# Attention with three DMA-joined pairs of blocks, values in half-blocks, and TensorE's program written out

## The reference

```python
dots = jnp.einsum('bhnd,bhmd->bhnm', q, k) * SCALE          # 2 x 16 heads, 2048 x 2048, head width 32
attn = jax.nn.softmax(dots, axis=-1)
out  = jnp.einsum('bhnm,bhmd->bhnd', attn, v)
```

## Time and profile before

| | us |
|---|---|
| median of three executions | 1948.23 |
| the profiled execution: its time | 1950.18 |
| the profiled execution: its span | 1948.4 |
| attention in it | about 318 to 1422 |
| TensorE busy | 1814.7 (93%) |
| VectorE busy | 1456.9 (75%) |
| ScalarE busy | 1448.6 (74%) |
| GpSimd busy | 161.3 (8%) |

### The profile page before, as it was taken

The page is one execution under the profiler, slowest core; times in us unless marked ns, Lnnn a source line. Parts: engine busy times, 40 slices in busy tenths (PEclk is TensorE's granted clock), DMA queues, the critical chain, the costliest instruction groups (busy, mean ns, idle before and its releaser), DMA issues. The chain is left out here.

```text
span 1948.4 us, 38894 instructions
## 1 busy us (share of the span) xinstructions
PE 1814.7 (93%) x14516; PEld 845.0 (43%) x14516; DVE 1456.9 (75%) x1579; ACT 1448.6 (74%) x1572; POOL 161.3 (8%) x131
## 2 busy tenths in 40 slices
PE   8999996999999999999999999999939996899786
PEld 6777772333333333333333333333327774444332
DVE  5443435888888888888888888888826776688687
ACT  5343445999999999999999999999905654555475
POOL 0000000000000000000000000000011220000164
PEclk9999998999999999999999999999969996899898
DMA  8655654536446364463555354463653520133274
GB/s 293 224 202 199 221 194 166 109 91 151 92 113 145 75 145 113 89 159 80 114 140 108 88 151 94 110 148 75 143 184 135 182 93 1 60 141 156 80 281 167
DMA packets 111553, 268.57 MB, mean 138 GB/s; under 512 B 7956, under 2 KB 26516, under 8 KB 101780
## 3 DMA queue, kind: packets, MB, share of 16 engines
q1 hardware_dynamic: 98324, 193.05, 27.4%
q0 software_dynamic: 9216, 67.11, 18.6%
q10 hardware_dynamic: 3968, 7.86, 1.1%
HBM read 115.95 MB, written 84.93 MB: 103 GB/s over the span
## 5 line engine op out<-in xcount | busy, mean ns | idle before, releaser
L783 DVE TENSOR_TENSOR dve_sum<-dve_sum,probs 128x2048 f32<-128x2048 f32 x320 | 732.8, 2290 | 80.7 <-ACT probs L699 73.1
L699 ACT ACTIVATE probs<-score_others,shift_now 128x1536 f32<-128x1536 f32 x384 | 622.0, 1620 | 0.0
L840 PE MATMUL score_first<-q_parts,k_parts 32*128 32x512 f32 x1542 | 494.1, 425 | 24.2 <-DMA v_group<-v_scratch 11.6
L840 PE MATMUL score_others<-q_parts,k_parts 32*128 32x512 f32 x4626 | 499.0, 426 | 0.0
L840 PEld LDWEIGHTS score_first<-q_parts,k_parts 32*128 32x128 f32 x1542 | 245.0, 183 | 492.2 <-ACT probs L698 288.0
L868 PE MATMUL mixed_ps<-probs,v_group 128*32 128x512 f32 x3072 | 395.9, 603 | 2.9
L698 ACT ACTIVATE probs<-score_first,shift_now 128x512 f32<-128x512 f32 x384 | 291.1, 758 | 43.0 <-PE score_others L840 43.0
L840 PEld LDWEIGHTS score_others<-q_parts,k_parts 32*128 32x128 f32 x4626 | 252.6, 183 | 2.2
L699 ACT ACTIVATE probs_joined<-score_others,shift_now 128x1536 f32<-128x1536 f32 x128 | 199.9, 1562 | 0.0
L812 POOL DMA_DIRECT2D probs_joined<-probs_joined x64 | 55.2, 863 | 1040.7 <-PE mixed_ps L868 1010.7
L868 PEld LDWEIGHTS mixed_ps<-probs,v_group 128*32 128x32 f32 x3072 | 67.1, 108 | 160.2 <-issue 110.0
(11 more groups left out here) (206 smaller groups left out, 2181.9 us busy)
## 6 DMA issues: line engine op xcount, KB each, us to landing
probs_joined<-probs_joined POOLq DMA_DIRECT2D x64, 1024.0 KB, 8.6
k_parts<-k_scratch SPq DMA_DIRECT2D x36, 512.0 KB, 4.8
q_parts<-q_scratch SPq DMA_DIRECT2D x33, 512.0 KB, 7.8
o_scratch<-out_parts SPq DMA_DIRECT2D x33, 512.0 KB, 2.8
h_scratch<-h SPq DMA_DIRECT2D x6, 2816.0 KB, 8.1
h<-h_scratch SPq DMA_DIRECT2D x6, 2816.0 KB, 10.5
k_scratch<-parts SPq DMA_DIRECT2D x32, 512.0 KB, 3.6
q_scratch<-parts SPq DMA_DIRECT2D x32, 512.0 KB, 2.7
```

Source lines behind the costliest of these rows:

```text
L699: nc.scalar.activation(block_probs(k)[:, CH:HPG * CH], score_others[n % 2][:], ACT.Exp, bias=shift[:, c:c + 1], scale=SCALE).then_inc(prob ...
L783: nc.vector.tensor_tensor(total[:], first[:], block_probs(k)[:], ALU.add).then_inc(dve_added, 1)
L840: last = nc.tensor.matmul(out, k_parts[rows, a, k * P:(k + 1) * P], q_parts[c][rows, b, :], start=t == 0, stop=t == len(TERMS) - 1)
```

## The change

Three pairs of blocks are now joined by DMAs: (0, 1), (4, 5) and (10, 11). Only the sum of the last goes to a ones-group of its own (`TO_SUMS`). The sums of the other two are read by VectorE as two of its twelve operands (`ADD_ORDER`), so that it still makes eleven additions. There are two ones-groups for each chunk instead of three: the joined pair in step 0, `dve_sum` in step 1 (`SUMS_AT`). VectorE reads the sums (`finish`) before its first addition of a chunk, no longer after it. The values are issued in halves of 256 columns: `VALUE_HALVES` says how many halves a step takes. Steps 2 and 3 take blocks 0 and 1. Steps 4, 7, 10 and 13 take three halves. Blocks 3, 4, 5, 10, 11 and 12 are split over two steps, the others are issued whole. The ring for single blocks has five tiles instead of six. `normal` is gone (the product is written into `mixed`), and `out_parts` is single instead of double, with one `stored` semaphore. TensorE's program has no loop: all 32 chunks are written out, and the two scores past the end are left out.

```diff
-    JOINED = (8, 9, 10, 11)
-    ADDED = [k for k in range(KB) if k not in JOINED]
-    ADDS = len(ADDED) - 1
-    P_RING = len(ADDED) // 2
+    PAIRS = ((0, 1), (4, 5), (10, 11))
+    TO_SUMS = (2,)
+    ADD_ORDER = (2, 3, 6, 7, 0, 8, 9, 4, 12, 13, 14, 15)
+    SUMS_AT = ((0,), (1,))
     W_SLOT = 4
+    SINGLE = [k for k in range(KB) if not any(k in pair for pair in PAIRS)]
+    ADDS = len(ADD_ORDER) - 1
+    P_RING = len(SINGLE) // 2
     AHEAD = 2
-    VALUES_AT = [[], [], [0], [1, 2], [3], [4, 5]] + [[k] for k in range(6, KB)]
+    VALUE_HALVES = (0, 0, 2, 2, 3, 2, 2, 3, 2, 2, 3, 2, 2, 3, 2, 2)
+    HALF = CH // 2
...
-            return probs_joined[JOINED.index(k)] if k in JOINED else probs[ADDED.index(k) % P_RING]
+            i = pair_of(k)
+            return probs[SINGLE.index(k) % P_RING] if i is None else probs_paired[i][PAIRS[i].index(k)]
+        def pair_of(k):
+            return next((i for i, pair in enumerate(PAIRS) if k in pair), None)
+        def added_at(k):
+            return max(ADD_ORDER.index(k), 1)
...
-                            if k in JOINED:
+                            i = pair_of(k)
+                            if i in TO_SUMS:
                                 act.wait_ge(sums_done, it * CPB + c + 2)
-                            elif ADDED.index(k) >= P_RING:
-                                act.wait_ge(dve_added, (it * CPB + c + 1) * ADDS + max(ADDED.index(k) - P_RING, 1))
+                            elif i is not None:
+                                act.wait_ge(dve_added, (it * CPB + c) * ADDS + added_at(PAIRS[i][0]))
+                            elif SINGLE.index(k) >= P_RING:
+                                act.wait_ge(dve_added, (it * CPB + c + 1) * ADDS + added_at(SINGLE[SINGLE.index(k) - P_RING]))
                             else:
-                                act.wait_ge(dve_added, (it * CPB + c) * ADDS + ADDED.index(k) + P_RING)
+                                act.wait_ge(dve_added, (it * CPB + c) * ADDS + added_at(SINGLE[SINGLE.index(k) + P_RING]))
...
+                        take_shift(it if c == 0 else it + 1, (c + CPB - 1) % CPB)
+                        finish(it, c)
                         for a in range(ADDS):
-                            k = ADDED[a + 1]
-                            n = c * KB + k
-                            if a == 1:
-                                take_shift(it if c == 0 else it + 1, (c + CPB - 1) % CPB)
-                                finish(it, c)
                             if a == ADDS - 1:
                                 gather(it, c + 1)
-                            v.wait_ge(probs_done, (it + 1) * EXPS + (n + 1) * 2)
+                            k = ADD_ORDER[a + 1]
+                            if pair_of(k) is None:
+                                v.wait_ge(probs_done, (it + 1) * EXPS + (c * KB + k + 1) * 2)
+                            else:
+                                v.wait_ge(joined[pair_of(k)], 16 * (it * CPB + c + 1))
                             if a == 0:
                                 v.wait_ge(sums_done, 1 + it * CPB + c)
-                                first = block_probs(ADDED[0])
+                                first = block_probs(ADD_ORDER[0])
...
-                for i in range(2):
-                    nc.gpsimd.memset(probs_joined[2 * i][:], 1.0).then_inc(filled, 1)
-                pool.sem_inc(joined, 2)
+                for i in TO_SUMS:
+                    nc.gpsimd.memset(probs_paired[i][0][:], 1.0).then_inc(filled, 1)
                 with pool.Fori(0, ITERS) as it:
                     for c in range(CPB):
-                        for i in range(2):
-                            pool.wait_ge(mixed_done, (it + 1) * BLOCKS + c * KB + JOINED[2 * i + 1] + 1)
+                        for i, pair in enumerate(PAIRS):
+                            pool.wait_ge(mixed_done, (it + 1) * BLOCKS + c * KB + pair[1] + 1)
                             pool.sem_inc(may_join, 1)
-                            nc.gpsimd.dma_start(probs_joined[2 * i][:], probs_joined[2 * i + 1][:], accum_op=ALU.add).then_inc(dma_joined[i], 16)
-                        for i in range(2):
-                            pool.wait_ge(dma_joined[i], 16 * (it * CPB + c + 1))
-                            pool.sem_inc(joined, 1)
+                            nc.gpsimd.dma_start(probs_paired[i][0][:], probs_paired[i][1][:], accum_op=ALU.add).then_inc(joined[i], 16)
+                for signal in joined:
+                    pool.wait_ge(signal, 16 * ITERS * CPB)
...
-                def sums(turn, c, at):
-                    f = turn * PAIR + c
+                def sums(f, at):
                     if at == 0:
                         pe.wait_ge(mixed_copied, f + 1)
-                        pe.wait_ge(filled, 2)
-                    if at < 2:
-                        pe.wait_ge(joined, 2 * f + at + 1)
+                        pe.wait_ge(filled, len(TO_SUMS))
+                    if at < len(TO_SUMS):
+                        part = probs_paired[TO_SUMS[at]][0]
+                        if f > 0:
+                            pe.wait_ge(joined[TO_SUMS[at]], 16 * f)
                     else:
+                        part = dve_sum[(f + 1) % 2]
                         pe.wait_ge(dve_added, (f + 1) * ADDS)
-                    part = (probs_joined[0], probs_joined[2], dve_sum[(c + 1) % 2])[at]
                     for j in range(HPG):
                         last = nc.tensor.matmul(mixed_ps[j * HD:(j + 1) * HD, :], keep.ones[:, 0:HD], part[:, j * CH:(j + 1) * CH],
-                                                start=at == 0, stop=at == 2)
-                    if at == 2:
+                                                start=at == 0, stop=at == len(TO_SUMS))
...
-                def values(turn, c, k):
-                    pe.wait_ge(probs_done, EXPS + turn * (2 * TURN_BLOCKS) + (c * KB + k + 1) * 2)
+                def values(f, k, halves):
+                    pe.wait_ge(probs_done, EXPS + (f * KB + k + 1) * 2)
                     if k == 0:
-                        pe.wait_ge(sums_read, 1 + turn * PAIR + c + 1)
+                        pe.wait_ge(sums_read, 1 + f + 1)
+                    lo, hi = halves[0] * HALF, (halves[-1] + 1) * HALF
                     for j in range(HPG):
-                        last = nc.tensor.matmul(mixed_ps[j * HD:(j + 1) * HD, :], v_group[:, k, j * HD:(j + 1) * HD],
-                                                block_probs(k)[:, j * CH:(j + 1) * CH], start=k == 0, stop=k == KB - 1)
-                    last.then_inc(mixed_done, 1)
+                        last = nc.tensor.matmul(mixed_ps[j * HD:(j + 1) * HD, lo:hi], v_group[:, k, j * HD:(j + 1) * HD],
+                                                block_probs(k)[:, j * CH + lo:j * CH + hi], start=k == 0, stop=k == KB - 1)
+                    if halves[-1] == 1:
+                        last.then_inc(mixed_done, 1)
...
-                with pe.Fori(0, TURNS) as turn:
-                    for c in range(PAIR):
-                        for step, blocks in enumerate(VALUES_AT):
-                            score(turn, c * KB + step + AHEAD)
-                            for at in ((0,), (1, 2))[step] if step < 2 else ():
-                                sums(turn, c, at)
-                            for k in blocks:
-                                values(turn, c, k)
-                for at in range(3):
-                    sums(TURNS, 0, at)
+                for f in range(CHUNKS):
+                    done = 0
+                    for step, halves in enumerate(VALUE_HALVES):
+                        if f * KB + step + AHEAD < CHUNKS * KB:
+                            score(f * KB + step + AHEAD)
+                        for at in SUMS_AT[step] if step < len(SUMS_AT) else ():
+                            sums(f, at)
+                        for k in range(KB):
+                            now = [half for half in range(2) if done <= 2 * k + half < done + halves]
+                            if now:
+                                values(f, k, now)
+                        done += halves
+                for at in range(len(TO_SUMS) + 1):
+                    sums(CHUNKS, at)
```

58 lines of the change are left out of this document (24 added, 34 removed).

## The result

The changed kernel takes 1980.39 us (median of four runs, 1975.28 to 1985.79), the kernel before 1948.21 beside it. The ratio is 1.0163, with a 95% interval from 1.0133 to 1.0192: 1.6% slower, where 0.65% faster was forecast. The profiled execution took 1985.79 and its span 1984.0.

The account below looks back on a forecast made before the run. Neither TensorE nor ScalarE bounds by its sum: uneven steps of one starve the other. Chunks of 33.8 for 34.13 give -10.2 and the end -2.4, together -12.6 from the 1948.2 median: 1935.6 us, range 1899 to 1949.

Parts of the forecast that it names:

- the term L = 8.0: Join of (10, 11), issue to landing: 8.0 us, bounds 7.0 and 8.3, with one load over every join.
- the sum: Whole kernel: 31 chunk periods of 33.8 instead of 34.13 give -10.2, the end -2.4, together -12.6 us.
- hidden with 1.3 to spare: VectorE's chain of eleven additions: ends at S1 + 30.1 to 30.7, before `gather` must start at S1 + 32.0.
- the 0.2 for the fetches: Instruction pages meeting the join of (10, 11): 0.2 us a chunk on average, bounds 0 and 1.0.
- The price of a half: TensorE's value groups: half a group costs 0.43 to 0.46 us, so triple steps take 2.33 to 2.36.
- the circle of the sum: From S1 (start of step 1's scores) through the join of (10, 11) to the next S1: 25.6 + L us.
- One sign of being right: VectorE at the end of its additions: it idles before `gather`.
- TensorE itself pays nothing: Written-out program's instruction fetches: no stall of TensorE's own, since no chunk was longer for the fetched pages.
- Dear halves: Rival on half-width rounds: at 0.34 us each they add 2.2 to a chunk, 36.1, total 2008; chance 0.04.
- Fetches on the critical join: Rival: a page in nearly every join of (10, 11), L = 9.0, chunk 34.6, total 1961; chance 0.11.
- VectorE as the bound: Sign of being wrong: VectorE late at `gather`, its additions waiting for pair (0, 1) or (4, 5); no size.
- The range: Whole kernel's time: 1899 to 1949 us, meant to leave out no more than two in ten.

Follow-up runs that it names:

- the kernel without both disturbances: Changed kernel with TensorE's program as a loop of two chunks and the third piece of keys and values after block 15's values: 1936.33 us, ratio 0.9932.
- the loop kernel: Changed kernel with TensorE's program as a hardware loop over two chunks, GpSimd relaying the landing of (10, 11), all else as changed: 1972.61 us, ratio 1.0125.
- The fill: the loop kernel plus two groups of thrown-away ones-matmuls in step 0 after every second chunk: 1960.01 us, ratio 1.0054.
- the fastest kernel: the kernel without both disturbances, with extra half-blocks in steps 4, 6, 9 and 11, so block 11 is done in step 11: 1911.12 us, ratio 0.9802.

## Why the prediction was wrong

Three steps failed: the term L = 8.0 of the join (10, 11), which was 9.4 to 11.1 in fourth chunks; TensorE's clock behind a long wait, which the sum had at nothing; and "hidden with 1.3 to spare" for VectorE's additions, together with the 0.2 for the fetches. The sum had 33.8 for every distance, 1081.6 in all. The changed kernel has 51.0 more: 8 x (37.86 - 33.8) = 32.5 in the fourth places, 13.5 in the seven chunks with a late (0, 1), 5.9 in chunks 0 to 2, and -0.9 in the 14 quiet ones.

*What held.* The price of a half is half (steps of 1.90 and 2.33; 2.33 to 2.36 was forecast). TensorE waits 1.45 in step 0 of a quiet chunk (1 to 1.5), ScalarE idles behind it, (10, 11) lands after 8.1 (8.0 to 8.5), and the chunk takes 33.7 (about 33.8). So the circle of the sum was right, and the kernel without both disturbances, 1079.5 and 1936.33, bears it out. One sign of being right did not hold even there: VectorE does not idle before `gather`.

*The term L in fourth chunks.* I took 8.0 with an upper bound of 8.3 from two joins, both in the earlier trace rows, and wrote that in every fourth chunk keys and values would lie over the join instead of the query load. In both of those joins that load was issued behind the join. I did not work out that the third piece waits for block 11 and the join for block 11 too, and that SyncE is the quicker to issue: 0.36 ahead. The kernel before has the same order at its second join of each fourth chunk, the 10.4 of the earlier trace rows; I did not set it beside SyncE's issues:

```profile
858.72 0.38 SPq L627 DMA_DIRECT2D k_parts<-k_scratch  x1
859.08 0.86 POOL L812 DMA_DIRECT2D probs_joined<-probs_joined  x1 [3.16 <-PE mixed_ps L868]
```

The run with the load 1.5 behind gave 8.3, the one with it 0.4 ahead 10.6. So the bytes were priced rightly and their place was not, by some 2.5 us in each fourth chunk.

*A term that was missing: TensorE's clock.* The sum let TensorE go on at its old pace after a wait. The quiet chunk's 1.45 us do it no harm; in the loop kernel, after 3.7 to 5.0 us, it resumed at 1.2 GHz. The fill took 1.96 from each fourth place, beside the 2.5 of the late join: together the 4.4 by which the loop kernel's fourth place (38.16) stood above its others (33.74).

*The fetches.* "TensorE itself pays nothing" held: outside steps 0 and 1, TensorE's steps are the same in the written-out kernel as in its loop. The gaps from the start of one block's last scores to the next block's first cluster at the same lengths (between 430 and 1420 us 295 of 1.3 to 1.5 us and 116 of 1.6 to 1.9 among 449, in the loop 306 and 114 among 454). The Trainium skill ("Runtime: NRT & Kernel Launch", Instruction fetch mechanics) says that fetching is hidden behind the issue of instructions, and these steps agree. Its advice to unroll does not hold here: the loop shows no stall, and the text costs. The term itself, 0.2 a chunk on (10, 11), had a wrong size and asked about one join only. In chunks 0 to 2 pages made (10, 11) land 1.0 to 1.4 later. More often they fell on (0, 1), whose sum VectorE reads. There "hidden with 1.3 to spare" failed: the spare was 1.0, a join 2 us later used it up, TensorE waited for the copy, and its clock fell in four of these seven chunks too. The text costs 8 us in the changed kernel, where other waits cover part of it, 25 where the loads are late, 31 in the fastest kernel, 12 in the kernel before. Why the same text costs the kernel before less was not tried; it has no join that VectorE reads.

*The edits in one step each.* Loop alone: 8 less. Third piece later alone: 19 less. Both: 44 less. They overlap: with one removed, the other still makes TensorE late. That is read from these sums, and was not tried chunk by chunk.

*The rivals.* Dear halves: no. Fetches on the critical join: its 1961 is the time of the written-out kernel with late loads (1961.37), but by luck: (10, 11) was late by a page in three of the first 24 places and not in nearly all, and the rest came through (0, 1) and the fourth chunks. VectorE as the bound was in the list of what would show me wrong, not among the rivals with a price. The range ended at 1949, because no case in it let two terms that share the path be wrong at once.

## What to carry to other kernels

When a transfer becomes critical, list every transfer issued in the microseconds around it and in which order they go out; if two wait for the same event, one of them will be ahead. Give each wait a second term, what its engine's clock does afterwards, and price a shortened spare time at each of its inputs and not only at the nearest one. A program text that is written out is not free where transfers have little to spare.

## What was not expected of the hardware

- A 1 MiB join within the on-chip memory takes 6.9 to 7.0 us where nothing is issued within 6 us behind it, 8.0 to 8.3 with 512 or 768 KB issued 1.1 to 2.8 behind it, and 10.2 to 10.9 with 768 KB of which the first 512 are issued 0.36 ahead (loop kernels, without pages).
- A page of 16 KB holds one DMA engine for about 1.04 us, but seven joins that it met landed about 2 us later (9.9 to 10.4 for 8.1). In these the last of the join's 16 packets of 4 bytes went only as the page ended, 8.8 to 9.4 us after the issue instead of 7.7. In 18 joins with a page at the same place it had gone by the page's start, and they landed after 8.1 to 8.9.
- After the eight waits of 2.7 to 6.8 us behind fourth chunks of the changed kernel TensorE's granted clock was 0.50, in chunk 7 until 611. After waits of 2.2 to 2.8 us in other chunks it was 0.50 in six of ten. After waits of 1.45 us it stayed at 1.00.
- A hardware loop over two chunks, some 770 matmuls and as many weight loads, needs three pages in 1040 us (seven in the fastest kernel), and its jump back shows no cost.
